# Turned scan orders read the straight orders' u and are scanned from the last column to the first; the scan loop runs over batches

## The reference

```python
s0 = _local_scan(xc, WSZ, False)          # 8 x 8 windows, rows first
s1 = _local_scan(xc, WSZ, True)           # columns first
xs = jnp.stack([s0, s1, s0[..., ::-1], s1[..., ::-1]], axis=1)
x_dbl = jnp.einsum('bkdl,kcd->bkcl', xs, x_proj_w)
dts, bs, cs = (x_dbl[:, :, :R], x_dbl[:, :, R:R + N], x_dbl[:, :, R + N:])
dts = jnp.einsum('bkrl,kdr->bkdl', dts, dt_projs_w)
delta = jax.nn.softplus(dts + dt_projs_b[None, :, :, None])
A = -jnp.exp(A_logs)
ys = _selective_scan(xs, delta, A, bs, cs, Ds)
y = _local_reverse(ys[:, 0], WSZ, h, w_, False) + _local_reverse(ys[:, 1], WSZ, h, w_, True) + _local_reverse(ys[:, 2, :, ::-1], WSZ, h, w_, False) + _local_reverse(ys[:, 3, :, ::-1], WSZ, h, w_, True)
```

## Time and profile before

| what | value |
|---|---|
| runs | 13180.49, 13187.52, 13191.48 us; median 13187.52 |
| profiled execution, its own time | 13188.5 us |
| its span, first to last instruction | 13186.6 us |
| busy: VectorE (DVE) | 11097.4 us (84%) |
| busy: GpSimd (POOL) | 9937.2 us (75%) |
| busy: TensorE (PE) | 8944.7 us (68%), mean granted clock 0.771 |
| busy: ScalarE (ACT) | 7096.2 us (54%) |
| DMA | 2060.69 MB, mean 156 GB/s |

### The profile page before, as it was taken

One profiled execution on the slowest core, in us unless ns is written; L12 is line 12 of the kernel. 1 busy time (PEld: TensorE's weight loads), 2 busy tenths in 40 slices (PEclk: granted clock), 3 DMA queues, 4 the chain that ended last, 5 costly groups with the idle time before them and its releaser, 6 DMA issues. The chain is left out here.

```text
span 13186.6 us, 117417 instructions
## 1 busy us (share of the span) xinstructions
PE 8944.7 (68%) x25624; PEld 2522.6 (19%) x25624; DVE 11097.4 (84%) x7002; ACT 7096.2 (54%) x9476; POOL 9937.2 (75%) x4196
## 2 busy tenths in 40 slices
PE   7866666666666666666666666666666664777777
PEld 2211111111111111111111111111111111222222
DVE  7769999999999999999999999999999995333333
ACT  6755555555555555555555555555555552444444
POOL 0029999999999999999999999999999994211220
PEclk9977777777777777777777777777777776888888
DMA  4567777777777777777777777777777784323230
GB/s 140 166 184 172 175 176 179 175 173 173 177 177 177 175 172 178 177 176 176 172 171 176 175 177 177 172 176 177 177 177 173 175 180 105 78 61 83 65 81 24
DMA packets 581902, 2060.69 MB, mean 156 GB/s; under 512 B 82662, under 2 KB 87654, under 8 KB 566886
## 3 DMA queue, kind: packets, MB, share of 16 engines
q1 hardware_dynamic: 581478, 2057.01, 68.1%
HBM read 1599.54 MB, written 457.18 MB: 156 GB/s over the span
## 5 line engine op out<-in xcount | busy, mean ns | idle before, releaser
L819 POOL TENSOR_TENSOR dBu<-rep,BC 128x1024 f32<-128x1024 f32 x3072 | 7152.8, 2354 | 963.0 <-DMA rep<-dd_dram 922.2
L615 PE MATMUL py<-hC,fold 128*32 128x512 f32 x12288 | 2958.3, 861 | 2587.5 <-POOL hC L826 2443.7
L664 ACT ACTIVATE pd<-rep,a_now 128x1024 f32<-128x1024 f32 x3072 | 3420.9, 1114 | 1326.4 <-DVE hC L787 1002.3
L779 DVE TENSOR_TENSOR_SCAN pd<-pd,carry,dBu 128x1024 f32<-128x1024 f32 x1536 | 3595.5, 2341 | 0.0
L826 POOL TENSOR_TENSOR hC<-h,BC 128x1024 f32<-128x1024 f32 x1024 | 2400.5, 2344 | 531.9 <-DVE h L779 484.7
L787 DVE TENSOR_TENSOR hC<-pd,BC 128x1024 f32<-128x1024 f32 x2048 | 2507.5, 1224 | 169.6 <-DVE pd L779 29.2
L779 DVE TENSOR_TENSOR_SCAN h<-pd,carry,dBu 128x1024 f32<-128x1024 f32 x768 | 1797.9, 2341 | 0.0
L676 ACT ACTIVATE carry<-pd 128x1 f32<-128x1 f32 x1536 | 262.0, 171 | 2630.2 <-DVE hC L787 2582.3
L615 PEld LDWEIGHTS py<-hC,fold 128*32 128x32 f32 x12288 | 516.8, 138 | 4803.9 <-POOL hC L826 3205.8
L779 DVE TENSOR_TENSOR_SCAN pd<-pd,dBu 128x1024 f32<-128x1024 f32 x512 | 1168.0, 2281 | 43.4 <-issue 28.3
L1385 POOL TENSOR_TENSOR p_yn<-p_yn,p_z 96x1024 f32<-96x1024 f32 x64 | 149.8, 2345 | 1192.3 <-DMA p_z<-zs_dram 774.8
(11 more groups left out here) (147 smaller groups left out, 9216.5 us busy)
## 6 DMA issues: line engine op xcount, KB each, us to landing
rep<-dd_dram SPq DMA_DIRECT2D x1024, 768.0 KB, 12.7
BC<-bc_dram SPq DMA_DIRECT2D x2048, 256.0 KB, 9.1
u_dram<-p_u SPq DMA_DIRECT2D x64, 1536.0 KB, 16.7
u<-u_dram SPq DMA_DIRECT2D x128, 768.0 KB, 5.4
dd_dram<-LG SPq DMA_DIRECT2D x256, 384.0 KB, 4.5
dd_dram<-RL SPq DMA_DIRECT2D x256, 384.0 KB, 3.0
y_dram<-y SPq DMA_DIRECT2D x256, 384.0 KB, 10.9
p_y<-y_dram SPq DMA_DIRECT2D x64, 1536.0 KB, 13.9
```

The costliest lines, as they stand in the source:

```text
L615: last = mm(py[32 * g:32 * g + 32, t2(t)], fold[:, :], hC[:, j % 2 * 3 + g, t2(t)], start=(j % 4 == 0), stop=(j % 4 == 3), skip_group_chec ...
L664: go(pd[:, i % 2, :], rep[:, half, 0, g, :], ACT.Exp, scale=a_now[:, i:i + 1]).then_inc(S.exped, 1)
L779: v.tensor_tensor_scan(dst, pd[:, i % 2, :], dBu[:, i % 4, :], carry[:, i:i + 1] if c else 0.0, ALU.mult, ALU.add).then_inc(S.scanned, 1)
L819: nc.gpsimd.tensor_tensor(dBu[:, i % 4, :], rep[:, half, 1, g, :], BC[:, s, 0, r, :], ALU.mult).then_inc(S.dbu, 1)
```

## The change

The tile U holds two orders instead of four. The copies on VectorE, their semaphores and the stores of orders 2 and 3 go. In the scan stage, orders 2 and 3 load the chunks of orders 0 and 1 in turned order (`stored_at`), and all work before the scan is done on straight columns. The scan's three operands (pd, dBu, and pd or h) get a negative step for k >= 2 (`turned`), and the kept state is column 0 instead of column 1023 (`last_of`). y is stored at the turned chunk's place, so that it lies straight in DRAM, and the output stage adds it with forward reads. As the direction must be known when the program is written, the loop now runs over 7 batches with 16 chunks written out, and the last batch stands behind it. `pick_a` gets k as a constant.

```diff
-        U = sb("p1_u", [C, K, L])
+        U = sb("p1_u", [C, 2, L])
...
             def store_u(b, h):
-                for k in (0, 1, 2, 3):
-                    sp.wait_ge(u_made[k], done((b * 2 + h + 1) * (NT if k < 2 else 1)))
+                for k in range(2):
+                    sp.wait_ge(u_made[k], done((b * 2 + h + 1) * NT))
...
-            for k in range(K):
+            for k in range(2):
                 sp.wait_ge(u_stored[k], done(16 * B * 2))
...
                 if t == 0:
                     act.wait_ge(u_stored[k], done((b * 2 + h) * 16))
-                    act.wait_ge(u_made[k + 2], done(b * 2 + h))
...
-            def reverse(b, h, k):
-                dve.wait_ge(u_made[k], done((b * 2 + h + 1) * NT))
-                dve.wait_ge(u_stored[k + 2], done((b * 2 + h) * 16))
-                nc.vector.tensor_copy(U[:, k + 2, :], U[:, k, ::-1]).then_inc(u_made[k + 2], 1)
-
...
-                    if s in (11, 13) and not first:
-                        reverse(b - 1, 1, (s - 11) // 2)
-                    if s in (21, 23):
-                        reverse(b, 0, (s - 21) // 2)
...
-            for k in range(2):
-                reverse(B - 1, 1, k)
...
+        def stored_at(bk, k, c):
+
+            return bk * NC + c if k < 2 else bk * NC + NC - 1 - c
+
+        def turned(row, k):
+
+            return row if k < 2 else row[:, ::-1]
+
+        def last_of(k):
+
+            return slice(T - 1, T) if k < 2 else slice(0, 1)
...
-            with eng.Fori(0, BK - 1) as bk:
+            with eng.Fori(0, B - 1) as b:
+                for k in range(K):
+                    for c in range(NC):
+                        body(b * K + k, k, c, NC)
+            for k in range(K):
                 for c in range(NC):
-                    body(bk, c, NC)
-            for c in range(NC):
-                body(BK - 1, c, NC - 1 - c)
+                    body(BK - K + k, k, c, NC if k < K - 1 else NC - 1 - c)
...
-                sp.dma_start(u[:, s, :, :], a.u_flat[m]).then_inc(u_loaded[s], 16)
+                sp.dma_start(u[:, s, :, :], a.u_flat[stored_at(bk - k // 2 * 2, k, c)]).then_inc(u_loaded[s], 16)
...
-                sp.dma_start(a.y_flat[n, :, half, :], y[:, half, :]).then_inc(y_stored[half], 16)
+                sp.dma_start(a.y_flat[place, :, half, :], y[:, half, :]).then_inc(y_stored[half], 16)
...
-            def pick_a(bk):
+            def pick_a(bk, k):
                 act.wait_ge(S.exped, done(bk * NC * NS))
-                act.sem_inc(S.passed, 1)
-                go(a_now[:, :], a_neg[:, bk % K, :], ACT.Identity).then_inc(S.a_picked, 1)
+                go(a_now[:, :], a_neg[:, k, :], ACT.Identity).then_inc(S.a_picked, 1)
...
-                    src = h[:, i // 3 % 2, T - 1:T]
+                    src = h[:, i // 3 % 2, last_of(k)]
...
-                    src = pd[:, i % 2, T - 1:T]
+                    src = pd[:, i % 2, last_of(k)]
...
-                v.tensor_tensor_scan(dst, pd[:, i % 2, :], dBu[:, i % 4, :], carry[:, i:i + 1] if c else 0.0,
-                                     ALU.mult, ALU.add).then_inc(S.scanned, 1)
+                v.tensor_tensor_scan(turned(dst, k), turned(pd[:, i % 2, :], k), turned(dBu[:, i % 4, :], k),
+                                     carry[:, i:i + 1] if c else 0.0, ALU.mult, ALU.add).then_inc(S.scanned, 1)
...
-                nc.gpsimd.tensor_tensor(Y[:, 0, :], Y[:, 0, :], Y[:, 2, ::-1], ALU.add).then_inc(S.y_sum02, 1)
+                nc.gpsimd.tensor_tensor(Y[:, 0, :], Y[:, 0, :], Y[:, 2, :], ALU.add).then_inc(S.y_sum02, 1)
...
-                nc.gpsimd.tensor_tensor(Y[:, 1, :], Y[:, 1, :], Y[:, 2, ::-1], ALU.add).then_inc(S.y_sum13, 1)
+                nc.gpsimd.tensor_tensor(Y[:, 1, :], Y[:, 1, :], Y[:, 2, :], ALU.add).then_inc(S.y_sum13, 1)
```

More of the change, by code:

```diff
@@ L468, in load_skip, with load_u @@
                 sp.dma_start(w_skip[:], a.w_skip[bk]).then_inc(S.skip_loaded, 16)
-            def load_u(m, s):
+            def load_u(bk, k, c, s):
+                bk, k, c = bk + (k + c // NC) // K * K - k + (k + c // NC) % K, (k + c // NC) % K, c % NC
+                m = bk * NC + c
                 sp.wait_ge(S.skipped, done((m - 1) * 2))
@@ L518, in load_rep, with store_y @@
                                  a.dd[half].rearrange("x (g d) t -> d (x g) t", g=3)).then_inc(rep_loaded[half], 16)
-            def store_y(n, half):
+            def store_y(n, half, place):
                 sp.wait_ge(S.y_made, done(n * 2 + half + 1))
                 sp.sem_inc(S.passed, 1)
-                sp.dma_start(a.y_flat[n, :, half, :], y[:, half, :]).then_inc(y_stored[half], 16)
+                sp.dma_start(a.y_flat[place, :, half, :], y[:, half, :]).then_inc(y_stored[half], 16)
             load_weights(0)
             load_skip(0)
-            load_u(0, 0)
-            load_u(1, 1)
+            load_u(0, 0, 0, 0)
+            load_u(0, 0, 1, 1)
             store_bc(0, 0)
@@ L533, in _, with body @@
             store_prep(0, 1)
-            def body(bk, c, left):
+            def body(bk, k, c, left):
                 n, s = bk * NC + c, c % 2
@@ L540, in body @@
                 if c > 0:
-                    store_y(n - 1, 1)
+                    store_y(n - 1, 1, stored_at(bk, k, c - 1))
                 if left:
@@ L545, in body @@
                     load_rep(n + 1, 0)
-                store_y(n, 0)
+                store_y(n, 0, stored_at(bk, k, c))
                 if left:
                     if left >= 2:
-                        load_u(n + 2, s)
+                        load_u(bk, k, c + 2, s)
                     if c == NC - 2 and left == NC:
@@ L555, in body @@
                 if c == NC - 1:
-                    store_y(n, 1)
+                    store_y(n, 1, stored_at(bk, k, c))
             chunk_loop(sp, body)
@@ L725, in _ @@
             act.wait_ge(S.a_ready, done(1))
-            pick_a(0)
+            pick_a(0, 0)
             for i in range(2):
@@ L737, in body @@
                     if c < NC - 1:
-                        save_state(bk, c, i)
+                        save_state(bk, k, c, i)
                     if left or i + 2 < NS:
                         if c == NC - 1 and i + 2 == NS:
-                            pick_a(bk + 1)
+                            pick_a(bk + 1, (k + 1) % K)
                         expo(*at(bk, c, i + 2))
@@ L763, in delta_u, with scan @@
                 v.tensor_tensor(du[:, :], pp[0:HALF, :], u[:, s, half, :], ALU.mult).then_inc(S.du_made, 1)
-            def scan(bk, c, i):
+            def scan(bk, k, c, i):
                 half, r, g = where(i)
@@ L793, in _, with body @@
             delta_u(0, 0, 1)
-            def body(bk, c, left):
+            def body(bk, k, c, left):
                 n, s = bk * NC + c, c % 2
                 for i in range(NS):
-                    scan(bk, c, i)
+                    scan(bk, k, c, i)
                     if where(i)[2] < 2:
```

5 lines of the change are left out of this document (2 added, 3 removed).

## The result

| | before | after | predicted |
|---|---|---|---|
| median of the runs | 13189.5 us | 12971.1 us (12968.03 to 12992.16) | 12997 (12950 to 13110) |
| ratio to before | | 0.9837, 95% interval 0.982 to 0.9854 | 0.986 |
| profiled execution, its own time | 13188.5 | 12992.2 | 12997.5 |
| its span | 13186.6 | 12990.3 | |

Measured a second time, the same kernel took 12972.8 us against 13191.6 (ratio 0.9837, 0.982 to 0.9853). By the medians the change brings 218 us, where 191 were forecast.

A forecast was written before the change was run, and what follows sets the result against it. VectorE bounds the scan stage, with GpSimd nearly as full. From 13188.5 us, 90 in the input stage and 101 at the scan loop's seams go, backward scans costing 0: 12997.5, or 12997 against the median; overall range 12,950 to 13,110.

The forecast's parts named there:

- narrower range: Whole kernel: the forecast's own range, 12,965 to 13,080 us, given chance 0.70.
- Input stage: -90 forecast: Input stage: 70.9 us of waits for z, 4.4 and 14.6 us go; 90 us, between 70 and 105.
- 4.4 forecast: Input stage, normalisation before the first of six waits: two copies precede it on VectorE and go, 4.4 us.
- 14.6 forecast: End of the input stage: two of three last stores of u go, 2 x 7.3 = 14.6 us.
- VectorE does not take z's place: Input stage: VectorE reaches the first normalisation four copies (8.8 us) and about 2.5 us earlier, keeping most of its 4.24 us slack.
- 24 x 4.21: Scan loop: 24 fewer jumps back, each priced by ScalarE's two issue gaps at 4.21 us; 101 us, bounds 37 and 115.
- the ends 1.56 and 4.21 us: Gain per seam without the jump: 1.56 us if TensorE's later handover is the rule, 4.21 us if ScalarE's whole delay goes.
- up to 24 us: TensorE, SP and GpSimd, with longer bodies, may newly pay a jump: 6 times some 4 us; taken as nothing.
- 0 and 0.67 us per scan: VectorE's 1536 backward scans: extra cost between 0 and 0.67 us each, 0 taken; slower-scans rival about 14,025 us, chance 0.12.
- estimate of 0.4 us per scan: Backward scans on VectorE: skill page's adjacent-pair rule would make each some 0.4 us slower, about 13,610 us in all.
- the 0.6 us of the text: Output stage: GpSimd's sums, now reading forwards, take at most 0.6 us more each; nothing in the sum.
- Rivals 2 and 3: 2: only copies and stores pay, seams do not, 13,098 us, chance 0.09. 3: only seams pay, about 13,087 us, chance 0.06.

The follow-up runs named there:

- batch loop alone: Kernel before with only the loop over batches changed; copies, four stores and straight scans stay: 13071.4 us, ratio 0.9909.
- loop over pairs: Kernel before with two orders in the loop's body, 14 jumps instead of 30: 13102.5 us, ratio 0.9946.
- copies kept: Kernel after with VectorE's 32 turned copies still made, but never stored or loaded: 13035.0 us.
- stores kept: Kernel after with 64 stores of u, the additional ones from the rows of orders 0 and 1, ScalarE waiting for them too: 13097.2 us.
- forward: Kernel after with every scan from first column to last, so orders 2 and 3 are scanned the wrong way round: 12971.8 us, ratio 0.9834.
- copy later: Kernel after with the last copy of y of orders 0 to 2, and its store, moved into the next order: 12898.6 us, ratio 0.9785.
- stores from own rows: Kernel after with 64 stores of u, the additional ones from rows filled with zeros once, ScalarE waiting for none of these: 13055.2 us.
- one step more: Kernel after with one semaphore step per order put back in ScalarE's body: 12973.6 us, ratio 0.9846.
- kernel without a loop: Kernel after with all eight batches of the scan written out: 12891.8 us, ratio 0.9772.

## Why the prediction was right, and where its sizes were off

The time came out 26 us below the forecast and just inside the narrower range (12,965 to 13,080). The gain of the scan stage, 127.1 us, lies above its upper bound of 115; the sum stayed in the range because the input stage was far from its own bound of 105.

**Input stage: -90 forecast, -89.8 measured.** The cause is shown by the experiments, but the terms are not quite the predicted ones. The squares' wait for z went from 70.9 to 17.6 us, not to 0. That is the bound the text named: the next half's stores of u are issued 7 us behind z (463.48 against 456.51), z lands after 17.0 us instead of 13.8, and 2.5 to 3.3 us of each wait stay. I had put 13 us on it in the range; it was 17.6. In exchange ScalarE's waits for old stores of u fell to 12.4 us, which I had left to the range. Before, they were:

```profile
ACT p_u L308 <- DMA u_dram<-p_u: 25.0, 9, 17.0
```

At the first of the six waits, the squares start 18.9 us sooner (202.0 against 220.9), of which the shorter wait is 13.4; the other 5.5 lie ahead of it (4.4 forecast). The end of the stage gives 23.16 - 7.84 = 15.3 (14.6 forecast). Sum: 53.3 + 12.6 + 5.5 + 15.3 = 86.7; 3.1 us are not placed. The close hit is in part luck: two errors of opposite sign, the 17.6 us that stayed and the 12.6 us that were not counted. (A slip of the text that decides nothing: four copies of 2.28 us are 9.1 us, not 8.8.)

The statement that VectorE does not take z's place held, but only because its copies went in the same change: with them kept, the stage is 45.2 us longer, although z is in time.

**Scan loop: -101 forecast, -127.1 measured.** The place and the cause are the predicted ones; the batch loop alone gives 121.5 of it. The term "24 x 4.21" was sized too small, in three ways:

- It took the six remaining jumps to cost what they did before. They cost 3.94 - 2.27 = 1.7 us instead of 4.0: 6 x 2.3 = 14 us.
- It gave straight code no other advantage than the missing jump. Three more orders stand behind the loop, each 3.0 us shorter: 9 us.
- It counted ScalarE's gaps alone. But VectorE has a gap of its own at a jump, "issue" before the first scan of the order. It stood in the earlier trace rows with 28.3 us and fell to 9.7, and the wait there for ScalarE from 8.3 to 1.8. Before, some jumps were also long, with 7.7 to 9.5 us from copy to scan instead of 6.2.

From VectorE's side the sum closes: the wait at h fell by 178.2 - 86.7 = 91.5 us, the two waits before scans into pd by 18.6 and 6.5, and the idle time before the product by 169.6 - 159.9 = 9.7. That is 126.3 of 127.1. The lesson is that the first of these is smaller than 24 x 4.21, and that I had read only ScalarE's gaps, not those of the engine that bounds the stage. In the kernel after, the price of a jump on VectorE is nearly all its own gap (9.7 us for 6 jumps, up to 1.7 each): the wait at h is then no longer than without a jump (2.45 and 2.47 us), as ScalarE's gap of 1.6 us runs beside it.

The batch loop alone lacks 5.6 of the 127.1 us, and not the 14 that its dearer jumps cost. In its trace only 2 seams have the slow projections (over 6 us), in the kernel after 7, at some 1.3 us each.

What stays at the seam is the wait for TensorE, as was said. Between the ends 1.56 and 4.21 us for one seam the upper one was the right choice: 6.24 - 2.27 = 3.97 measured at the typical seam. The 4.19 us of idling in the earlier trace rows, from which the lower end was made, are a seam with slow projections: TensorE took 6.80 us for them from 10690.34, with a granted clock of 0.50, and 5.29 us at the seam of the earlier trace rows. Of the other engines' jumps, for which the text gave up to 24 us, GpSimd's showed as 3.8 us before its product, 6 times, and not on the path as far as the waits tell.

**Why a jump costs 4.0 or 1.7 us.** ScalarE has two issue gaps at a jump in every kernel with a loop: one of about 1.6 us behind the branch, and a second one a few instructions later. What differs is where the second one stands. It stands ahead of the exponential for which VectorE waits, with 2.2 us or more, in the kernel before, the batch loop alone, the loop over pairs, copies kept and stores kept. It stands two instructions later, behind that exponential, with 1.0 to 1.4 us, in the kernel after and in forward, copy later, stores from own rows and one step more. All of the first kind have additional waits in ScalarE's code of the input stage, ahead of the loop, and none of the second. The body's length does not decide it: the kernel with one step more stays at 1.7. The nearest pair are the two kernels with stores kept: on ScalarE they differ by these waits alone, which stand ahead of the loop, and have 4.0 and 1.7. So the place of the body in ScalarE's program goes with the price. That was seen in ten kernels and was not set by an experiment made for it; the cause stays argued. The Trainium skill (Runtime: NRT & Kernel Launch, "Instruction fetch mechanics") says that instructions come in blocks of 256 and that a branch out of the fetched ones stalls; this would explain a second gap that depends on where the body begins. No run here shows the blocks. The traces agree with its advice to unroll: no jump is left in the kernel without a loop, and it is 81 us faster than the kernel after, though most of that is not the jumps.

**Backward scans: 0 forecast, 0 measured.** The choice between 0 and 0.67 us per scan rested on the copy that read backwards, and held for writes and for PSUM too. The Trainium skill (Vector Engine (DVE) Microarchitecture Reference) calls negative steps unmeasured, in the section "Performance modes — why throughput varies by op and dtype" and not in the one that the prediction names. The estimate of 0.4 us per scan, which the prediction made from the rule on adjacent pairs in "Measured stream behaviour on trn2", does not hold here: the means agree to 1 ns. It was also high for that page's 2.5 ns per column, since 2.56 us for 1024 columns are only 0.2 to 0.3 us above the measured scans. The scan's own pace of 2.2 ns per element may cover a slower stream; that is not separated. The strided sum with 1.85 ns per element was the wrong neighbour.

**Output stage: 0 forecast.** It moved by +18.9 us in one execution and -6.9 in the other of the same program, so nothing is shown beyond chance. GpSimd's two sums, now with forward reads, take 8815 and 8839 ns, against 8832 and 8872: the 0.6 us of the text, worked out as four times a shorter product, did not appear.

**Rivals 2 and 3** fall with the two parts of the table: both the input stage and the scan stage gained. Rival 2 was put against by the seam before the last order alone, and that one row was enough: at all 24 new seams it is 2.26 or 2.27 us from copy to scan, as there.

## What to carry to other kernels

- An "issue" gap at the loop's edge has a price that can be read by comparing a seam with the jump to one without. Multiply it by the jumps that go, but read the gaps on the bound engine too and add up the result there. Expect the remaining jumps to change their price when the code moves: a gap costs less once it stands behind the instruction for which the bound engine waits.
- A loop costs more than its jumps. If the program may be long, compare one period of straight code with one in the loop: here 3.0 us in 310, or 84 us over the 28 orders in the loop. The register steps behind it can be read in the trace.
- Where two engines are both a few us behind the same transfer, take the work off both: one alone brings less than its share. And at a seam, give a copy that waits for another engine a later place than the work for which the bound engine waits.

## What I had not expected of the hardware

- The same jump back costs 4.0 us or 1.7 us, with the same body. ScalarE's second gap, of 1.0 us or more, stands ahead of the exponential in one case and behind it in the other; the kernels of the two kinds differ in waits ahead of the loop.
- In a loop VectorE starts the product behind some scans 0.09 us later than in straight code (2.46 against 2.37 us), with a register step of 40 ns in between.
- Eight projections of TensorE took 5.29 us at most seams and 6.63 to 6.65 us at seven of the kernel after, where its granted clock stayed longer at 0.50. VectorE, which bounds the stage, idled 1.3 us longer there.
- A scan with negative steps on all three operands, PSUM among them, takes the same 2341 and 2281 ns as a forward one, and a sum on GpSimd is no faster with forward reads (8815 and 8839 ns for 4096 elements against 8832 and 8872).
- A store of z of 3 MB landed after 13.7 us in the first batch, where the next stores came 12 us behind it, and after 17.0 to 17.2 us in the other seven, where two stores of u came 7 us behind: they cost it some 3.3 us. In the kernel before it was 25.7 us (median), with four stores of u ahead and four behind.
